# Two kinds of copies of an attention layer, issued from ScalarE's queue in place of the sync engine's

## The reference

```
q, k, v = split_heads(x @ Wq.T), split_heads(x @ Wk.T), split_heads(x @ Wv.T)
w   = softmax(q @ k.T / sqrt(8))        # over 256 keys, per head and query
out = merge_heads(w @ v) @ Wo.T
```

## Time and profile before

| what | value |
|---|---|
| median of 3 runs | 1626.0 us (1621.2 to 1633.96) |
| the profiled execution: its own time | 1636.59 us |
| its span | 1634.8 us |
| TensorE, busy share of the span | 71% |
| VectorE | 58% |
| ScalarE | 38% |
| GpSimd | 31% |
| granted clock of TensorE, mean | 0.835 |

### The profile page before, as it was taken

The page is one execution under the profiler, slowest core; times in us unless marked ns, Lnnn a source line. Parts: engine busy times, 40 slices in busy tenths (PEclk is TensorE's granted clock), DMA queues, the critical chain, the costliest instruction groups (busy, mean ns, idle before and its releaser), DMA issues.

```text
span 1634.8 us, 32039 instructions
## 1 busy us (share of the span) xinstructions
PE 1164.4 (71%) x9203; PEld 836.9 (51%) x9203; DVE 954.8 (58%) x3446; ACT 613.6 (38%) x1352; POOL 498.9 (31%) x711
## 2 busy tenths in 40 slices
PE   1498897889468888466644888989887698428840
PEld 1255554555257777355532666767655476326520
DVE  3476886786512222797753565667647688752227
ACT  1165554556233333234510454555555332103210
POOL 5111333433524444332451011111103211443553
PEclk9697887889689999798766899999997799559975
DMA  4223333230245556411103222222101000133422
GB/s 127 71 73 72 80 87 80 77 81 29 93 139 171 159 169 209 151 51 36 33 13 86 61 67 69 67 66 64 38 24 34 23 27 13 43 102 102 127 71 87
DMA packets 120631, 129.59 MB, mean 79 GB/s; under 512 B 14274, under 2 KB 104131, under 8 KB 117315
## 3 DMA queue, kind: packets, MB, share of 16 engines
q1 hardware_dynamic: 112834, 113.75, 24.7%
q0 software_dynamic: 7680, 14.37, 2.5%
HBM read 72.42 MB, written 36.00 MB: 66 GB/s over the span
## 4 chain that ended last, share of the span: by engine, by line
PE 36%; DVE 18%; issue 16%; DMA 14%; POOL 6%; SPq 4%; ACT 3%; another core or an unknown queue 2%; DVEq 1%; POOLq 0%; ACTq 0%
PE po L439 6%; DMA we<-in_pack 4%; DMA xr<-xg 4%; PE po L1492 3%; DVE xg L335 3%; PE pt L399 2%; PE pt L402 2%; PE pt L1486 2%; DMA xs<-xg 2%; POOL rstd L328 2%; PE pm L420 2%; PE pm L1486 2%; DMA scr<-parts 2%; PE pm L426 2%
## 5 line engine op out<-in xcount | busy, mean ns | idle before, releaser
L608 DVE TENSOR_REDUCE mx<-pm 128x2 f32<-128x512 f32 (+1 forms) x512 | 307.1, 620 | 243.7 <-PE pm L426 136.7
L561 ACT ACTIVATE ex<-pt 128x512 f32<-128x512 f32 (+1 forms) x512 | 271.5, 544 | 265.9 <-PE pt L399 132.9
L325 POOL TENSOR_SCALAR ve<-mv 128x2 f32<-128x2 f32 x96 | 25.5, 266 | 601.4 <-DVE mv L319 601.4
L1565 POOL DMA_INDIRECT result<-ye,to_row x144 | 135.7, 942 | 190.8 <-issue 147.2
L439 PE MATMUL po<-ex,va 128*32 128x256 f32 (+1 forms) x2048 | 163.9, 395 | 4.5 <-ACT ob L570 3.6
L402 PE MATMUL pt<-hide_k,ident 128*128 128x128 bf16 x512 | 97.7, 229 | 37.4 <-issue 28.4
L399 PE MATMUL pt<-qs,ks 99*128 99x256 bf16 x512 | 112.0, 307 | 14.9 <-DMA qs<-mt 10.8
L420 PE MATMUL pm<-ks,qs 96*128 96x256 bf16 x512 | 115.7, 313 | 6.3 <-DVE mx L608 5.5
L1492 PE MATMUL po<-he,we 128*128 128x256 f32 (+1 forms) x448 | 113.3, 396 | 5.8 <-DVE yt L1532 4.0
L304 PE MATMUL p<-ident,xs 128*128 128x128 f32 x112 | 40.1, 358 | 99.1 <-DMA xs<-xg 83.5
L309 ACT COPY xt<-p 128x256 f32<-128x256 f32 x112 | 41.8, 373 | 182.9 <-PE p L305 163.0
(11 more groups left out here) (281 smaller groups left out, 2808.8 us busy)
## 6 DMA issues: line engine op xcount, KB each, us to landing
we<-in_pack SPq DMA_DIRECT2D x40, 514.5 KB
xs<-xg SPq DMA_DIRECT2D x112, 128.0 KB
scr<-parts SPq DMA_DIRECT2D x32, 384.0 KB
we<-in_pack SPq DMA_DIRECT2D x16, 512.0 KB
qs<-scr SPq DMA_DIRECT2D x32, 192.0 KB
ks<-scr SPq DMA_DIRECT2D x32, 192.0 KB
yr<-result SPq DMA_DIRECT2D x48, 128.0 KB, 2.2
xe<-sorted SPq DMA_DIRECT2D x40, 132.0 KB
```

Source lines behind the costliest of these rows:

```text
L561: nc.scalar.activation(ex[j % 2][:, 2 * u:2 * u + 2, lo:S], pt[:, u, :].rearrange("p (b k) -> p b k", k=S)[:, :, lo:S], ACT.Exp).then_inc( ...
L608: nc.vector.tensor_reduce(mx[q.slot % 2][:, qt, 4 * b + 2 * u:4 * b + 2 * u + 2], pm[:, u, :].rearrange("p (b k) -> p b k", k=S)[:, :, 0:h ...
L1565: pool.indirect_dma_start(out=rows, out_offset=bass.IndirectOffsetOnAxis(ap=to_row[q.slot][0:m, i:i + 1], axis=0), in_=ye[q.slot][0:m, i, ...
```

## The change

The two issues leave SP's program. The maximum rows are issued by ScalarE right behind its copy to `mt`, after a wait for the end of that copy. The routing copy is issued by ScalarE in the step in which the sequence is at(6), at j = 0, behind the two exponentials of that j and ahead of the copy to `xt`. Its two waits go with it. ScalarE's sweep of layer 0 gets lead = SLOTS, so its loop begins later and covers fewer steps.

```
 heads_sync:
-                if (q := at(4)):
-                    sp.wait_ge(mt_sb, a + q.n + 1)
-                    for t in range(2):
-                        sp.dma_start(qs[q.slot][MAX_AT:MAX_AT + 3, :, t * P:t * P + P],
-                                     mt[q.slot % 2][STACK * t:STACK * t + STACK, :]).then_inc(mrows[q.slot], 16)
...
-                if routed and (q := at(6)):
-                    wait_apart(sp, ln_x, 2 * (n + q.n + 1), passed)
-                    wait_apart(sp, scattered[q.slot], 64 * q.turn, passed)
-                    for c in range(2):
-                        sp.dma_start(xr[q.slot][:, c, :, 0:D], xg[:, bass.ds(2 * q.n, 2), :]
-                                     ).then_inc(xr_loaded[q.slot], 16)
 heads_scalar:
                     if (q := at(3) if j >= T0 else at(4)):
                         exps(q, (j - T0) % 8)
+                    if routed and j == 0 and (q := at(6)):
+                        wait_apart(act, ln_x, 2 * (q.n + 1), passed)
+                        wait_apart(act, scattered[q.slot], 64 * q.turn, passed)
+                        for c in range(2):
+                            nc.scalar.dma_start(xr[q.slot][:, c, :, 0:D], xg[:, bass.ds(2 * q.n, 2), :]
+                                         ).then_inc(xr_loaded[q.slot], 16)
                     if j == 0 and (q := at(0)):
                         copy_xt(act, q, g)
                     if j == 1 and (q := at(3)):
...
                         nc.scalar.copy(mt[q.slot % 2][:, :], p0[0:96, S:2 * S].bitcast(BF16)[:, 0:P]
                                        ).then_inc(mt_sb, 1)
+                        wait_apart(act, mt_sb, a + q.n + 1, passed)
+                        for t in range(2):
+                            nc.scalar.dma_start(qs[q.slot][MAX_AT:MAX_AT + 3, :, t * P:t * P + P],
+                                                mt[q.slot % 2][STACK * t:STACK * t + STACK, :]
+                                                ).then_inc(mrows[q.slot], 16)
...
-            sweep(act, 8 if routed else 6, step, lead=1 if routed else 0)
+            sweep(act, 8 if routed else 6, step, lead=SLOTS if routed else 0)
```

## The result

The changed kernel takes 1643.2 us (median of 10 runs, 1636.2 to 1655.0), the kernel before 1625.8 us (10 runs on the same chip). The ratio is 1.0112, 95% interval 1.0082 to 1.0142: slower by 1.1%. The range of the forecast (1555 to 1645) holds it; the forecast itself, 1624, had the wrong sign.

The account below looks back on a forecast made before the run. Bound taken: layer 0's cycle of waits, with the routing copy held behind the stack, and late maximum rows in layer 2. Layer 0 -2, layer 2 -1 and +2, fills -1: -2 us together, forecast 1624, range 1555 to 1645.

Parts of the forecast that it names:

- Step (4): Copies beside the stack: single packets take turns on busy engines, so the routing copy ends with the stack, as now.
- rival A: Copies pass the stack, layer 0's waits open, layer 2's long steps become short: 63 us saved, 1563 us; chance 0.30.
- the ring: Layer 0: stack delays routing copy, that delays TensorE's L495, which releases `parts` and the next stack; 23.2 us a step.
- Step (2): ScalarE's added issues: 3.0 us a step in layer 0, 0.9 felt by TensorE; 0.1 to 0.2 felt in layer 2.
- Cover gone: +9: Layer 0: ScalarE's 0.9 us a step hide under the wait before L495, costing 0; without that wait, +9 us.
- ring as now, 0.2 us less in ten steps: Layer 0: the cycle of waits stays, 0.2 us shorter in ten steps because part of the copy has passed: -2 us.
- -1 for the late rows: Layer 2: late maximum rows now pass `xs`, saving 1 us.
- fills: -1: Filling of the pipeline: 1 us saved.
- Step (3): Layer 0: ScalarE issues the routing copy at 262.0 us where SP did at 259.39, 2.6 us later.
- Rival C: Layer 0: routing copy still takes 11.6 us from a 2.6 us later issue, in 11 steps: +29, 1655 us; chance 0.12.
- Rival D: The change doesn't do what it says, for instance the queue is shared all the same: 1626 us; chance 0.05.
- B: Copies pass the stack but ScalarE pays in full, 3.0 us a layer-0 step, 1.5 in layer 2: 1600 us; chance 0.08.

Follow-up runs that it names:

- scalar_held: Kernel before, both copies left on SP, ScalarE doing idle writes of about the issues' length in their places: 1.0015 of the kernel before.
- first_held: Kernel before with SP issuing the routing copy ahead of `scr` and the stack, plus ScalarE's idle writes; no copy on ScalarE's queue: 0.9898 of the kernel before.
- after_gated: Changed kernel with SP again waiting for ScalarE's `mt` copy before issuing `scr`: 1.0129 of the kernel before.
- lead_only: Kernel before with only lead = SLOTS in ScalarE's sweep of layer 0, no copy moved: 0.9993 of the kernel before.
- split_first: Kernel before with the stack in DMAs of eight rows and SP's routing copy issued ahead of `scr` and the stack: 0.9683 of the kernel before.
- changed_again: The changed kernel measured once more, on another chip: 1.0089 of the kernel before.

## Why the prediction was wrong

Step (4), that the copies don't pass the stack: right, and by its own mechanism. Single packets take turns on the two busy engines, the copy's last runs land with the stack, L483 still waits for `xr`, and rival A didn't come. But A was right that the ring could be opened; what opens it is the place in the order (0.983 on SP's queue, 0.990 on ScalarE's), not the queue.

Step (2), ScalarE's issues (but see below): 1.41 and 1.62 us a step against 1.4 and 1.6 forecast. What TensorE feels of them in layer 0 is 3.7 us in 9 steps before L451 and 3.1 us in 10 before L387 (142 to 390 us of the changed kernel), 0.7 us a step against 0.9. That most of it falls under the wait for the routing copy held too, as far as idle writes show it: 0.15% by `scalar_held`. "Cover gone: +9" was 0.65%, 10.7 us of 1652, in `first_held` (8.0 us between the two medians). In layer 2 a short step pays 0.1 to 0.2 us, as forecast.

The step that failed is the sum, in its terms for the moved copies: "ring as now, 0.2 us less in ten steps", so -2 (4), "-1 for the late rows" and "fills: -1". They have the wrong sign. (The "value: 0" for what SP loses, step (1), held as far as `after_gated` shows it.) Step (3) put the routing copy's issue 2.6 us later; against the stack it came 3.4 us later, and the turns gave 2.4 back. So the ring's DMA part became longer, from 16.9 to 17.8 us a step, where the sum had it 0.2 us shorter. I had reckoned only when the copies' own packets would be through beside the stack, and let the rest of the ring run as if nothing had changed. Between the two profiles these terms measured +9 in ten steps of layer 0, +7 in its fill and +10 in the long steps of layer 2. Against `lead_only`, which moves no copy, they are +4 to +6, +3 to +6 and +0.5 to +4 in the two profiles of the changed kernel.

By the ratios, which are the firmer measure, the whole change costs 0.9 to 1.1%, 15 to 18 us. ScalarE's idle writes are 0.15% of it, 2 to 3 us. The other 0.75 to 0.95%, 12 to 16 us, comes with the moved copies. How much of this is their queue, the routing copy's later issue or ScalarE is not settled. For the rows this term may belong to step (2) after all: I took an issue of 1.6 us for 1.6 us of ScalarE, of which 0.63 were idle before; with its gaps on either side it put the exponential off by 1.2 us.

Rival C had the right sign. It wanted 11.6 us from the later issue, +29; the trace has 10.6 us from issue to reading, in the step shown and in the mean of ten, so the copy still lands with the stack and 0.9 us a step is lost, not 2.6. It says nothing of the maximum rows. Rival D is out by the row of q10, B by the wait for `xr` that is still there.

The Trainium skill (DMA: Bandwidth & Descriptors, Rules for kernel authors) was weighed as the rule that spreading over queues saves issue time alone. The runs agree that nothing is gained (1.0112); beyond the rule, SP's saved issue time is spent on ScalarE. By the other rule that I cited from the Trainium skill (DMA: Bandwidth & Descriptors, Queues, rings and completion order, 9 to 17 descriptors of a queue before the next) rival A should have come. For this copy it didn't: the trace has one run of 512 B between two packets of 8 KB.

What stays open: why ScalarE's time costs 0.65% with the ring open, when it costs 0.15% with it closed and 1.2% on top of the whole change. The waits show cover being used up, but not where it ends. Whether the routing copy costs anything by itself, and if so by the queue or by the later issue; a kernel in which SP issues it 3.4 us later would tell. Whether the rows' 0.5% is their queue or ScalarE's time; a write that waits for the `mt` copy as the issue does would tell. And how the price is divided between the fill, layer 0 and layer 2: two profiles differ by up to 16 us in a stage that no edit touches.

## What to carry to other kernels

A copy that waits behind a big transfer is helped by being issued earlier, not by another queue: the routing copy's place in the order gained 1.7%, and moving it and the rows to a second queue lost 1.1%. Before you hide an engine's new work under a wait, count how much of that wait is spoken for: 3 us a step of idle writes cost 0.15% in the kernel before and over 1.2% on top of the change. A layer without such a wait has only the engine's own idle time to give: in layer 2, 1.6 us were nearly free and the next 1.6 us cost 0.9 us a short step. Compare a profile with a second one of unchanged code before you book its differences: here 6 us of a layer's 11 were spread. In a ring of waits "as now" is a forecast like any other; give it a size and a sign, and look for what can lengthen the ring before you look for what can open it.

## What was not expected of the hardware

- Two DMA issues of 1.62 us put the next exponential off by 1.20 us, an idle write of 1.69 us by 0.86. The issue begins 0.1 us after the copy ahead of it has ended (the program makes it wait for that end) and the next instruction 0.1 us after the issue; the write, which waits for nothing, overlaps both neighbours by 0.1 us. But two issues of 1.31 us behind an exponential put the `xt` copy off by 1.0 us, a write of 1.46 us by 1.4: the issues began 0.4 us before the exponential ended.
- Where two hardware queues had work for the same busy DMA engine, it took one run of 512 B from one and one packet of 8 KB from the other in turn (5 and 6 packets between 256 and 257 us of the changed kernel's profile).
- Cutting the stack into DMAs of eight rows, twice as many issues on SP, made the kernel 2.8% faster; with the routing copy first, 3.2% (`split_first`, 1584.25 us against 1634.59).
- The second experts' stage takes 93.0 us in one profile and 77.0 in another at the same clock of 1.00, in kernels that are the same there (`lead_only` 75.9, `changed_again` 96.8), with TensorE busy for 78.7 and 75.8 of it.
